# Perceiver-style stack on one core: inverse roots of layer norms and head norms by a GpSimd power and a Newton step, in place of ScalarE roots and reciprocals

## The reference, cut to what matters

```python
def _layernorm(x, axis=-1, eps=1e-05):
    m = jnp.mean(x, axis=axis, keepdims=True)
    v = jnp.var(x, axis=axis, keepdims=True)
    return (x - m) / jnp.sqrt(v + eps)

x = x + _L0_xattn_ref(_layernorm(x), ctx_768, ...)   # cross attention, 16 heads, 1601 keys of width 192
x = x + _L0_attn_ref(_layernorm(x), ...)             # causal self-attention, 64 positions
x = x + _L0_ffn_ref(_layernorm(x), ...)              # 256 -> 1024 -> 256, gelu
x = x + _L1_xattn_ref(_layernorm(x), ctx_768, ...)   # cross attention, 8 heads of 64
x = x + _L1_attn_ref(_layernorm(x), ...)             # a small network trained step by step over 16 batches
x = x + _L1_ffn_ref(_layernorm(x), ...)              # layer norm again, router, 2 of 8 experts, shared expert
```

## Time and profile before

| | |
|---|---|
| median of 3 runs | 2025.08 us (2022.79 to 2030.99) |
| profiled execution | 2025.8 us, its span (first to last instruction) 2023.4 us |
| PE busy | 1854.5 us, 92% |
| DVE busy | 1290.0 us, 64% |
| ACT busy | 940.3 us, 46% |
| POOL busy | 868.7 us, 43% |

### The profile page before, as it was taken

One profiled execution on the slowest core, in us unless ns is written; L12 is line 12 of the kernel. 1 busy time (PEld: TensorE's weight loads), 2 busy tenths in 40 slices (PEclk: granted clock), 3 DMA queues, 4 the chain that ended last, 5 costly groups with the idle time before them and its releaser, 6 DMA issues.

```text
span 2023.4 us, 43759 instructions
## 1 busy us (share of the span) xinstructions
PE 1854.5 (92%) x17682; PEld 1563.0 (77%) x17682; DVE 1290.0 (64%) x2725; ACT 940.3 (46%) x2016; POOL 868.7 (43%) x938
## 2 busy tenths in 40 slices
PE   5999999999999489677999999999999979789998
PEld 4788788888887368577999999999999946456665
DVE  4788888888888565434766667676676635642222
ACT  4666666666766233434444444444444425302222
POOL 4777777777776431205333333233333013202322
PEclk9999999999999698797999999999999989879999
DMA  5121121112101100122233222233222060131110
GB/s 149 35 67 35 34 59 44 35 35 67 35 3 54 43 1 1 50 56 62 58 88 84 58 58 58 58 88 84 58 58 58 1 272 19 55 122 24 26 28 16
DMA packets 50406, 113.04 MB, mean 56 GB/s; under 512 B 4848, under 2 KB 36928, under 8 KB 48672
## 3 DMA queue, kind: packets, MB, share of 16 engines
q1 hardware_dynamic: 45792, 105.13, 17.7%
q0 software_dynamic: 4416, 5.12, 1.5%
HBM read 105.78 MB, written 5.37 MB: 55 GB/s over the span
## 4 chain that ended last, share of the span: by engine, by line
PE 75%; DVE 10%; ACT 7%; issue 3%; DMA 3%; POOL 1%; SPq 0%; POOLq 0%; DVEq 0%; ACTq 0%
PE ps L104 8%; PE ps L163 7%; PE ps L2165 6%; PE ps L480 5%; PE ps L462 4%; PE ps L1366 4%; PE ps L439 4%; PE ps L2189 3%; DMA wsb<-in_ctxT 3%; PE ps L1367 3%; PE ps L456 2%; PE ps L390 2%; PE ps L1352 2%; PE ps L1351 2%; PE ps L1354 2%
## 5 line engine op out<-in xcount | busy, mean ns | idle before, releaser
L537 DVE TENSOR_REDUCE arena<-ps 128x1 f32<-128x400 f32 (+1 forms) x512 | 257.5, 565 | 93.6 <-PE ps L439 93.6
L668 ACT ACTIVATE arena<-ps 128x384 f32<-128x384 f32 (+1 forms) x512 | 223.3, 524 | 102.5 <-PE ps L462 102.5
L1366 PE MATMUL ps<-arenaR 128*128 128x386 f32 x768 | 246.2, 356 | 1.1 <-DVE arenaR L1453 1.1
L740 POOL TENSOR_TENSOR arena<-arena 128x512 f32<-128x512 f32 (+1 forms) x160 | 208.2, 1301 | 89.2 <-ACT arena L668 80.4
L1552 ACT CAST arenaR<-ps 128x512 fp32r<-128x512 f32 (+1 forms) x256 | 116.5, 507 | 226.0 <-PE ps L163 225.9
L1595 POOL TENSOR_TENSOR arenaR<-h,arenaR 128x400 fp32r<-128x400 f32 (+1 forms) x60 | 57.8, 964 | 374.7 <-ACT arenaR L1537 374.7
L1367 PE MATMUL ps<-arenaR 128*128 128x256 f32 x768 | 215.4, 280 | 0.0
L1453 DVE TENSOR_TENSOR arenaR<-ps,arenaR 128x512 fp32r<-128x512 f32 (+1 forms) x256 | 138.8, 584 | 25.8 <-ACT arenaR L1552 25.6
L1435 DVE TENSOR_TENSOR arenaR<-wsb,arenaR 64x400 fp32r<-64x400 f32 x64 | 66.0, 1035 | 137.1 <-ACT arenaR L1538 137.1
L1366 PEld LDWEIGHTS ps<-arenaR 128*128 128x128 f32 x768 | 145.1, 189 | 1.4 <-DVE arenaR L1453 1.4
L1367 PEld LDWEIGHTS ps<-arenaR 128*128 128x128 f32 x768 | 146.0, 190 | 0.0
(11 more groups left out here) (329 smaller groups left out, 4745.9 us busy)
## 6 DMA issues: line engine op xcount, KB each, us to landing
wsb<-in_ctx SPq DMA_DIRECT2D x16, 1152.0 KB
arena<-in_ctxT SPq DMA_DIRECT2D x16, 800.5 KB, 5.5
arena<-in_ctxT SPq DMA_DIRECT2D x32, 400.2 KB, 7.2
wsb<-in_ctxT SPq DMA_DIRECT2D x32, 400.2 KB, 7.6
gu<-in_m_gu SPq DMA_DIRECT2D x8, 1536.0 KB, 19.9
h<-in_ctxT SPq DMA_DIRECT2D x15, 800.5 KB, 5.2
dn<-in_m_dn SPq DMA_DIRECT2D x8, 768.0 KB, 9.3
wsb<-in_f_w SPq DMA_DIRECT2D x2, 1024.0 KB, 5.9
```

The lines of the kernel that those rows point to most:

```text
L537: e.tensor_reduce(mx4[n % 2][:, u, i:i + 1], ps[:, at("look", n, i, u), 0:400 + (i == 3)], AX.X, ALU.max).then_inc(c.maxed.at((n, i, u)), 1)
L668: e.activation(v[:, u, 0:128 * GN[s]], ps[:, at("st", n, s, u), 0:128 * GN[s]], ACT.Exp).then_inc(c.exp_a.at((x0, n, s, u)), 1)
L740: e.tensor_tensor(acc_p[0:k], acc_p[0:k], v[0:k, :, 128 * t:128 * t + 128], ALU.add).then_inc(added_p.at((n, s)), 1)
L1366: e.matmul(o, PTh[:, t, :], v[:, t, 0:386], start=(t == 0), stop=False)
```

## The change

`norm_act` is gone, and with it every Sqrt. In its place `norm_pool` raises the variances to the power -0.5 on GpSimd: a TENSOR_TENSOR with the operation pow, whose second operand is a column `half` that holds -0.5, broadcast. `inverse_root` on VectorE then makes one Newton step, y' = y (1.5 - 0.5 v y y), in three small ops that each wait for the last. VectorE waits for the power where it waited for the root. For `sa` the two roots of the layer norm and the root mean square become one: the power is taken of (1 + 1.19e-7) v + 1e-5 x 1.19e-7. The head norms do the same with 128x96 numbers: maximum with 1e-24 of the squared lengths on VectorE, power on GpSimd, Newton on VectorE.

In GpSimd's list the power stands first in the stages `sa`, `ff`, `x1`, `tt` and `mo`, before its splits or memsets; in `x0` it stands behind the weight splits and before the context's. The head norms' powers stand before `normalise(0)` and `normalise(4)`. GpSimd waits for its own power to be finished before it goes on.

```diff
+def power_pool(c, e, w, y, v, event):
+    w.wait_ge(*c.dv(("to root", event)))
+    w.wait_ge(*c.po("half"))
+    e.tensor_tensor(y, v, c.half.broadcast_to(list(v.shape)), ALU.pow).then_inc(c.root.at(event), 1)
+    w.wait_ge(*c.root(event))
+
+def inverse_root(c, e, w, y, v, s, event):
+    w.wait_ge(*c.root(event))
+    e.tensor_tensor(s, v, y, ALU.mult).then_inc(c.dv.at(), 1)
+    w.wait_ge(*c.dv.now())
+    e.scalar_tensor_tensor(s, s, -0.5, y, ALU.mult, ALU.mult).then_inc(c.dv.at(), 1)
+    w.wait_ge(*c.dv.now())
+    e.scalar_tensor_tensor(y, s, 1.5, y, ALU.add, ALU.mult).then_inc(c.dv.at(("rooted", event)), 1)
+
+EPS, RMS_EPS = 1e-5, 1.1920929e-07
+
 def norm_dve(c, e, w, tag, rms=False):
     w.wait_ge(*c.dv.now())
-    e.tensor_scalar(c.ve, c.mv[:, :, 1], 1e-5, None, ALU.add).then_inc(c.var.at(tag), 1)
-    w.wait_ge(*c.root(tag))
-    e.reciprocal(c.rs, c.sd).then_inc(c.dv.at(), 1)
     if rms:
...
+        e.tensor_scalar(c.ve, c.mv[:, :, 1], 1.0 + RMS_EPS, EPS * RMS_EPS, ALU.mult, ALU.add).then_inc(c.dv.at(("to root", tag)), 1)
+    else:
+        e.tensor_scalar(c.ve, c.mv[:, :, 1], EPS, None, ALU.add).then_inc(c.dv.at(("to root", tag)), 1)
+    inverse_root(c, e, w, c.rs, c.ve, c.sd, tag)
     w.wait_ge(*c.dv.now())
...
-def norm_act(c, e, w, tag, rms=False):
...
+def norm_pool(c, e, w, tag):
+    power_pool(c, e, w, c.rs, c.ve, tag)
@@ first stage, ScalarE
             split(0, i)
-        norm_act(c, e, w, x0)
@@ first stage, GpSimd
+        e.memset(c.half, -0.5).then_inc(c.po.at("half"), 1)
         e.memset(c.zeros[:, :], 0.0).then_inc(c.po.at("zeros"), 1)
         for k in ("wk", "wv"):
             w.wait_ge(*w_hi(k))
             e.tensor_tensor(wl[k], W[k], wh[k], ALU.subtract).then_inc(w_lo.at(k), 1)
+        norm_pool(c, e, w, x0)
         for i in range(4):
             split(0, i)
@@ selfattn, VectorE
         def norms(half):
             u = slice(4 * half, 4 * half + 4)
-            w.wait_ge(*roots(half))
-            e.tensor_scalar(s2[:, u, :], s2[:, u, :], 1e-12, None, ALU.max).then_inc(c.dv.at(), 1)
-            w.wait_ge(*c.dv.now())
-            e.reciprocal(s3[:, u, :], s2[:, u, :]).then_inc(inv.at(half), 1)
+            w.wait_ge(*sq_sum(4 * half + 3))
+            e.tensor_scalar(s2[:, u, :], s1[:, u, :], 1e-24, None, ALU.max).then_inc(c.dv.at(("to root", ("heads", half))), 1)
+            inverse_root(c, e, w, s3[:, u, :], s2[:, u, :], s1[:, u, :], ("heads", half))
@@ selfattn, ScalarE: norms(half) with its Sqrt, norm_act and their three calls are removed
@@ selfattn, GpSimd
         def normalise(t):
-            w.wait_ge(*inv(t // 4))
+            w.wait_ge(*c.dv(("rooted", ("heads", t // 4))))
...
+        def norms(half):
+            u = slice(4 * half, 4 * half + 4)
+            power_pool(c, e, w, flat(s3[:, u, :]), flat(s2[:, u, :]), ("heads", half))
+
         ended(w)
+        norm_pool(c, e, w, sa)
         for i, j in ((0, 0), (0, 1), (1, 0), (1, 1)):
             split_w(i, j)
         e.memset(vx[:, :, :, 64:65], 1.0).then_inc(ones.at("in"), 1)
         for t in range(NT):
+            if t % 4 == 0:
+                norms(t // 4)
             normalise(t)
@@ ffn, xattn, memory, moe: norm_act leaves ScalarE's list, norm_pool follows ended(w) in GpSimd's
```

More of the change, by code:

```diff
@@ L129, in __init__ @@
         self.st, self.mv = cc(128, NT, 6), cc(128, NT, 2)
+        self.half = cc(128, 1)
         self.ve, self.sd, self.rs = cc(128, NT), cc(128, NT), cc(128, NT)
-        self.ss2 = cc(128, NT)
         self.xs_d = nc.dram_tensor("h_rows", (128 * 9, D), F32, kind="Internal").ap()
@@ L139, in __init__ @@
         self.dv, self.ac, self.po = self.sig("dve_own"), self.sig("act_own"), self.sig("pool_own")
-        self.var, self.root, self.normed = self.sig("var"), self.sig("root"), self.sig("normed")
+        self.root, self.normed = self.sig("root"), self.sig("normed")
         self.hT_turned, self.hT_act, self.hT_dve = self.sig("hT_turned"), self.sig("hT_act"), self.sig("hT_dve")
@@ L822, in selfattn @@
     qkv, qk_out, sq_out, v_out, sq_sum = c.sig("qkv"), c.sig("qk_out"), c.sig("sq_out"), c.sig("v_out"), c.sig("sq_sum")
-    roots, inv, k_unit, q_unit = c.sig("roots"), c.sig("inv"), c.sig("k_unit"), c.sig("q_unit")
+    k_unit, q_unit = c.sig("k_unit"), c.sig("q_unit")
     q_turn, k_turn, q_take, k_take = c.sig("q_turn"), c.sig("k_turn"), c.sig("q_take"), c.sig("k_take")
@@ L1043, in project @@
             e.copy(vx[:, t, :, 0:64], ps[:, bank(t, 3), :].rearrange("p (a c) -> p a c", c=64)).then_inc(v_out.at(t), 1)
[L1045 to L1048, removed]
         def take_k(t):
@@ L1073, in act @@
         split_w(0, 0)
-        norm_act(c, e, w, sa, rms=True)
         for i, j in ((0, 1), (1, 0), (1, 1)):
@@ L1082, in act @@
             project(t)
-        norms(0)
         for t in range(4, NT):
             project(t)
-        norms(1)
         take_k(0)
@@ L1190, in act @@
         e.copy(w2h, m.fw2).then_inc(w_hi.at("w2"), 1)
-        norm_act(c, e, w, ff)
         for n in range(4):
@@ L1206, in pool @@
         ended(w)
+        norm_pool(c, e, w, ff)
         for k, v, hi, lo in (("w1", m.fw1, w1h, w1l), ("w2", m.fw2, w2h, w2l)):
@@ L1560, in act @@
         ended(w)
-        norm_act(c, e, w, x1)
         for i in range(4):
@@ L1621, in pool @@
         ended(w)
+        norm_pool(c, e, w, x1)
         for i in range(4):
@@ L1974, in act @@
         ended(w)
-        norm_act(c, e, w, tt)
         take_h_act(c, e, w, tt)
@@ L2018, in pool @@
         ended(w)
+        norm_pool(c, e, w, tt)
         for v in (flat(z[64:128]), flat(gram[64:128]), minus[64:128], W2T[64:128], hg[64:128], da[64:128], dr[64:128], hs[0][64:128], hs[1][64:128]):
@@ L2415, in act @@
         ended(w)
-        norm_act(c, e, w, mo)
         w.wait_ge(*routing("logits"))
@@ L2449, in pool @@
         ended(w)
+        norm_pool(c, e, w, mo)
         e.memset(C_[:, :, NS:NS + 1], 0.0).then_inc(c.po.at("past the last"), 1)
```

## The result

| | median | lowest to highest | runs |
|---|---|---|---|
| before | 2024.28 us | 2022.79 to 2030.99 | 4 |
| after | 2064.80 us | 2056.63 to 2067.16 | 4 |

The ratio is 1.0186, 95% interval 1.015 to 1.0223. The change costs 1.9%. Forecast were 2030 us and a range of 2019 to 2056; the median lies above both. The profiled execution took 2065.14 us, its span 2063.3.

What follows compares the result with a forecast made beforehand. The chain, 75% TensorE, was taken to bound the kernel. Terms -0.75 - 0.5 + 6.9 - 1.3 + 0.8 - 0.7 + 0 = +4.5 us gave 2030 us, range 2019 to 2056.

Steps and rivals of the forecast that it cites:

- the price of the power: GpSimd's power: 0.2 us plus c = 36 ns for each element of a partition, 0.5 us for 8, 3.7 for 96.
- 2p - 0.5: Head norms: VectorE waits for two powers of p each, both on the chain; 6.9 us lost for p = 3.7.
- the sum of 4.5: All stages' terms together: +4.5 us; in general total = -3.45 + 216 c, c in us.
- feed-forward: Its layer norm: Newton done before GpSimd's first split, 1.3 us gained if the power stays under some 1.2 us.
- Rival (1): Head norms: the power is dear and VectorE waits twice; from c = 63 ns slower by over 10 us; chance 0.39.
- Rival (2): The power costs what a TENSOR_TENSOR does, c = 2.2 ns: -3.0 us, 2023; chance 0.12.
- Rival (3): A table switch costs 1.28 us more at each of five exposed places, power cheap: -9.4 us; chance 0.04.
- First stage: Normalised rows seven microseconds earlier gain nothing; the load before the first Exp goes if the initial table holds Exp: 0.75 us gained.
- Self-attention's layer norm: One Newton op before GpSimd's split 0, two behind splits; 0.5 us gained, bounds 0 to 1.2.
- Memory: Memory layer's norm: the power goes ahead of GpSimd's nine memsets, moving them and L191's tiles later: 0.8 us lost.
- Experts: Experts' layer norm: from variances to L191 1.2 us in place of 1.88, 0.7 us gained.
- Second cross attention: The stage waits for its context ten microseconds past the norm, so the change there gives 0.

Runs made afterwards that it cites:

- the head norms alone: Against the changed kernel, layer norms go back to ScalarE's roots, head norms keep power and Newton step: 2058.89 us, ratio 1.0155.
- the layer norms alone: Against the changed kernel, head norms go back to ScalarE's root and VectorE's reciprocal, the six layer norms keep power and Newton step: 2029.13 us, ratio 1.0006.
- The cheap operation: Against the kernel with later head-norm Newton steps, GpSimd subtracts in place of the power in self-attention's and feed-forward's layer norms: 2024.36 us.

## Why the prediction was wrong, step by step

**The step that failed is the price of the power.** "I take sixteen passes, c = 36 ns, nearer the cheap row": it measured 159 ns, and 0.39 us fixed in place of 0.2. The bounds of 2.2 and 220 ns held, the choice between them did not; the nearest row was that of an op of another kind, a single arithmetic step, and being the only one it drew the estimate to it. By its own rule the text said that from 63 ns on the kernel would be slower by over 10 us, and it gave that a chance of 0.39.

**The mechanism was right.** Head norms "2p - 0.5" is 30.7 us at p = 15.62, and the two waits measured 31.0. With VectorE not standing there, the whole loss was gone; with a cheap operation in the same place, too. Without its prices the sum of 4.5 is 4.5 - 3 x 0.5 - 2 x 3.7 = -4.4; with 3 x 1.66 and 2 x 15.62 put in, it is +31.8. What the sum lacked is added here:

| | us |
|---|---|
| the sum of the prediction at the measured prices | +31.8 |
| TensorE's lower clock behind the first gap, a term that the sum does not have | +2.5 |
| feed-forward, +0.6 at L1182 in place of -1.3 | +1.9 |
| the load ahead of the first Exp, no gain | +0.75 |
| left over, of 39.9 between the spans | 3.0 |

The 3.0 left over are differences between single executions as far as the runs show: the 2.15 behind the scores are not there in the head norms alone, the second cross attention was 1.4 shorter, and 0.7 of the experts' 1.2 are not in the sum either.

**Rival (1)**, the dear power, is what happened, at 159 ns. It gave 2055 at 150 ns, and the range ended there. At 159 its rule says 2057, and the median is 2065: beside c the upper end would have needed the terms in the table. Rival (2) fell with c. Rival (3), loads that cost twice, is not borne out: it would put the kernel with the layer norms alone some 3.5 us below before (the terms of its stages as measured, +2.9, less 6.4), and its interval ends at -1.6.

**First stage.** The rows come at 13.68 us instead of 20 and change nothing, as said. The load ahead of the first Exp is gone, so the table loaded at the start holds Exp, and the one before Tanh is gone too. The first Exp now starts 0.13 us behind the first scores, where it was 0.78, so the load's time is gone at that place. But the scores themselves came 0.84 us later (50.31 against 49.47), the Exp 0.19 later, and the stage took as long as before; that the load was worth its 0.75 us is not shown. The first power took 1.67 us, and the first context split began at 15.09 us, where it was 15.12. The Trainium skill ("GPSIMD Engine Reference", Instruction dispatch) puts about 6 us on the first call of a freshly loaded kernel. No row after shows it: the first power started 0.1 us behind GpSimd's weight splits.

**Self-attention's layer norm.** The locks fell as foretold: one Newton op before split 0, two behind splits. The front ended 0.9 us later, and "each microsecond more in the power costs one" makes -0.5 + 1.16 = +0.7 of it. At the first projection it was 0.43; the rest came from the clock, which rose 1.4 us later.

The Trainium skill ("SBUF — State Buffer", Who interferes with whom) says that a VectorE op with two SBUF inputs contends with a GpSimd instruction that reads SBUF, and not with one that only writes it. The splits (2.22 and 4.40 us) and the memsets (0.17 us) agree with it; the power, which reads SBUF, does not, as masks of 0.69 us passed within its 16.07. There the measurement decides.

**Feed-forward.** The step was to hold "as long as the power stays under some 1.2 us", and it took 1.64. The Newton ops then stood behind both splits, 4.40 and 4.42 us. The cheap operation showed the step right under its condition.

**Memory, experts, second cross attention.** Memory: 0.8 + 1.16 = 2.0 foretold at the measured price, the stage took 2.2 more, and memsets stop no Newton op. Experts: -0.7 + 1.16 = +0.5; from the variances to L205 it took 2.65 us in place of 2.05, +0.6. Second cross attention: hidden, as said.

**What the median adds.** The prediction's signs for the layer norms were a matter of a microsecond here and there; the layer norms alone measured +2.2 us with an interval that holds zero.

## What to carry to other kernels

Before an engine's list is made to wait for an operation that no trace of the kernel has, measure that operation at its size, or place the wait where there is work ahead of it: the same power cost 32 us right behind its input and nothing that could be measured three tiles later. When an op is short alone and long beside another engine, hold the other engine's side work back until the chain is past; here that gave 0.85%, with the power as well as with roots at the head of ScalarE's list, and 0.5% with the roots where they stood. A range for an unknown price should take the upper bound as seriously as the estimate when one row alone, of a simpler kind of operation, speaks for the lower.

## What the hardware showed that I had not expected

- A power on GpSimd costs 0.159 us for each element of a partition and 0.39 us fixed (1.66 us for 128x8, 4.15 for 128x24, 15.62 for 128x96), against 0.35 us for a product of 128x96.
- The power does not keep two-input VectorE ops out: masks of 128x512 took 0.69 us each while it ran, and 1.59 us where one started beside a product. The power beside them was 0.45 us longer (16.07 against 15.62).
- Newton ops of 128x8 beside a split last as long as the split (2.2, 4.4 us), beside memsets 0.17 us.
- After an idle stretch of 14.9 us TensorE came back at 1.2 GHz for 6 us, matmuls 0.43 us apart in place of 0.23. Behind the second gap it stayed there for 26.9 us, but so it did in the kernel before, behind 6.3 idle microseconds, for 19.0; across the kernels that time (18.8 to 26.9 us) did not go with the length of the gap.
